# A Flamingo-style block in one kernel: PSUM banks taken in turn, bf16 pairs in the second attention's output products, and another order of the first key and query chunks

## The chip, the cores and the metric

The kernel runs on one core of one Trainium2 chip, as a single launch. The metric is the device time of that core in microseconds, as the median of several runs. A core has five engines with an instruction queue each: TensorE (PE in the profile, PEld for its weight loads), VectorE (DVE), ScalarE (ACT), GpSimd (POOL) and SyncE (SP), which starts the DMAs. They meet through semaphores only. TensorE writes to PSUM, eight banks of 128 x 512 fp32 values, called BK0 to BK7 here.

## What is computed

Four batches of 256 tokens with 256 features pass through two layers; the context has 1601 vectors of 128 features in each batch. Cut to its lines, the reference is

```
x = x + tanh(g_xattn[0]) * L0_xattn(layernorm(x), ctx)        # 16 heads of 16, normed q and k
x = x + tanh(g_ffn[0])   * L0_ffn(layernorm(x))               # 16 experts, top 8, squared relu
x = x + tanh(g_xattn[1]) * L1_xattn(layernorm(x), ctx, mask)  # 16 heads of 128, 8 key heads
x = x + tanh(g_ffn[1])   * L1_ffn(layernorm(x))               # ternary weights, silu(up) * gate

# L1_xattn, of which the change touches the last two steps
q, k, v = text @ Wq, vision @ Wk, vision @ Wv                 # k and v shared by two heads
p   = exp(q . k / sqrt(128) - max)                            # over 1601 keys
out = (p @ v) / p.sum()
return out.reshape(B, 256, 2048) @ Wo
```

## The kernel before

A planner (class `Plan`) writes one list of pieces, such as `("sc", s)` or `("o1p", g, j)`. Each engine then goes through this list and issues its own share of each piece, so that the list sets the order on every engine. `fill(bank, piece)` gives a piece a PSUM bank, and the piece waits until the last user of that bank has been read. The waits are semaphores: `filled` (TensorE has written) and `emptied` (the reader is done).

- **Start (`first_batch`)**: keys and queries of batch 0 are projected into 16 tiles, which go on in five chunks: three of four key tiles (numbers 0, 1, 2 of the code), one of two key tiles (3, the tail), and one of the two query tiles (4). Each chunk is squared on ScalarE (`sq`), summed on VectorE (`ss`), square-rooted on ScalarE (`sqrt`), scaled on VectorE (`scale`), turned by TensorE (`kt`, for queries `qt`), copied twice by ScalarE (once as bf16) and split into a bf16 pair (`ksplit`, `qsplit`, L1528 on VectorE or L2069 and L2085 on GpSimd). Then rearranging matmuls (`qr`, `kr`) bring queries and keys to their places. The queries go through this last.
- **First attention (75 to about 515 us)**: tiles of scores (`sc`), exponentials on ScalarE (L1879), products with the values, and row maxima (`mx`, L1533 on VectorE). The banks 4, 0, 5, 1, 3, 2, 7 are taken in turn by `mbank`; bank 6 accumulates. When a group of heads ends, `finish` uses bank 7 outside this turn: `oB` (four transposes; VectorE reads them in L1561), `oC`, `oD` (VectorE in L1582) and the next norm's transposes `ln`. The router and the shared expert (`routed`) use bank 3 for the first half of the tokens.
- **Experts (about 515 to 620)**: 32 steps. `up` fills banks 0 to 2 and 3 to 5 in alternation; ScalarE (L1933, L1935) and VectorE (L1660, L1664) work on them; `dn` accumulates in bank 6. Everything else goes through bank 7: `routed` of the second half, 16 times `fold` (the second attention's weights multiplied together; ScalarE reads them in L1919 and L1920, and GpSimd splits the query side M1 into a bf16 pair in L2102 and L2104), four `tl` of the first half (VectorE in L1670), and norms. The maxima of the first two query groups of the second attention follow, with `md` always in bank 4 (read in L1993) and `mb` always in bank 5 (read in L1696).
- **Second attention (about 640 to 1436)**: 32 groups g of 13 steps, one for each 128 keys (`kt` is the step in the group). A step has three or four 128x512 bf16 matmuls of scores (`s1`), exp on ScalarE (L1981), a split on GpSimd (L2141), a running sum of the exponentials on VectorE in bank 6 (L1718 and L1721), and three matmuls with the context (`v1`) into bank 2 or 3. Maxima of later groups lie between. When a group ends, ScalarE copies the products (`o1v`, L2000) and the sums (`o1s`, L2006) out as fp32; `o1a` sums over partitions with four fp32 matmuls of one column; `o1p`, twice in a group, multiplies with the folded output weights N1 in two fp32 matmuls of 256 columns each, and VectorE adds the result to x (L1735).
- **Last feed-forward (to the end)**: not touched but for what runs ahead of it.

An fp32 matmul stands in the trace as two records. TensorE's instructions carry line L732, that of the helper `mm`.

## Time and profile before

| | |
|---|---|
| Median of 3 runs | 1485.71 us (1482.29 to 1487.23) |
| Profiled execution, its time | 1487.37 us |
| Its span in the profile | 1486.1 us |
| Busy: PE, DVE, ACT, POOL | 1356.2, 1025.3, 894.9, 680.9 us |
| Mean granted TensorE clock | 0.962 |

The span begins with the first instruction and ends with the last one; 1.3 us lie around it. Times of day below are microseconds from its start. Matmuls are pipelined, so the mean time of one is longer than the distance from one to the next; the busy time of a group is that of its union. A granted clock of 1.00 is 2.4 GHz, and 0.5 would be 1.2 GHz.

### The profile page before, as it was taken

To read this page: it belongs to the slowest core of one execution; us is meant where nothing else is said; L and a number is where in the kernel's file an instruction comes from. 1 tells how busy PE (TensorE), PEld (TensorE's weight loads), DVE (VectorE), ACT (ScalarE), POOL (GpSimd) and SP (SyncE) were. 2 spreads that over 40 slices of the span, in tenths; PEclk is the share of its full clock that TensorE was granted. 3 is DMA by queue.
4 is the path that set the end of the run, shared out by engine and by line. 5 is a ranking of instruction groups with operands and counts; after the bars stand their busy time and mean duration, and the time that the engine had idled before them with its cause. 6 is when DMAs were issued, how large, how long until landed. Compare 5 with 4: busy or idle time off the path is not lost.

```text
span 1486.1 us, 24911 instructions
## 1 busy us (share of the span) xinstructions
PE 1356.2 (91%) x8524; PEld 675.7 (45%) x8524; DVE 1025.3 (69%) x2259; ACT 894.9 (60%) x1575; POOL 680.9 (46%) x753
## 2 busy tenths in 40 slices
PE   5688979889878988789999999999999999999998
PEld 4243434334333344335455545545454555454555
DVE  5677787687787256756766666756667776767656
ACT  4656657557655756366665666555665555656554
POOL 4035343243040023157655547565576565555553
PEclk8799989999989999889999999999999999999999
DMA  4000301201250100001000000000010000000000
GB/s 174 1 1 15 77 2 24 46 1 28 42 199 1 58 0 6 23 23 29 1 1 1 23 1 24 6 1 23 1 29 29 1 30 1 30 1 1 1 2 29
DMA packets 20484, 36.66 MB, mean 25 GB/s; under 512 B 4898, under 2 KB 15238, under 8 KB 19334
## 3 DMA queue, kind: packets, MB, share of 16 engines
q1 hardware_dynamic: 20358, 35.07, 8.1%
q8 instruction: 68, 1.11, 0.3%
q14 instruction: 58, 0.48, 0.1%
HBM read 26.53 MB, written 1.15 MB: 19 GB/s over the span
## 4 chain that ended last, share of the span: by engine, by line
PE 50%; issue 3%; DVE 2%; ACT 2%; POOL 2%; DVEq 0%; POOLq 0%; ACTq 0%
PE BK L732 50%; POOL arena L2141 1%; DVE arena L1696 1%; DVE arena L2330 0%; ACT arena L1981 0%; ACT arena L1993 0%; DVE arena L2336 0%; POOL arena L1104 0%; PE BK L1377 0%; ACT L1024 0%; PE BK L1051 0%; ACT arena L2362 0%; ACT arena L2366 0%; POOL arena L2132 0%; POOL arena L1102 0%
## 5 line engine op out<-in xcount | busy, mean ns | idle before, releaser
L732 PE MATMUL BK<-arena 128*128 128x512 bf16 (+13 forms) x8194 | 1314.9, 365 | 94.5 <-DVE arena L1533 17.2
L732 PEld LDWEIGHTS BK<-arena 128*128 128x128 bf16 (+7 forms) x8194 | 639.9, 110 | 737.8 <-issue 193.2
L2141 POOL TENSOR_TENSOR arena<-arena 128x512 bf16<-128x512 f32 (+1 forms) x416 | 440.0, 1062 | 244.5 <-ACT arena L1981 187.0
L1981 ACT ACTIVATE arena<-BK,arena 128x512 f32<-128x512 f32 (+1 forms) x416 | 285.7, 687 | 199.0 <-PE BK L732 193.8
L1879 ACT ACTIVATE arena<-BK 128x512 f32<-128x512 f32 (+1 forms) x416 | 222.8, 601 | 116.7 <-PE BK L732 114.4
L1533 DVE TENSOR_REDUCE arena<-BK 128x1 f32<-128x512 f32 x384 | 241.3, 683 | 59.0 <-PE BK L732 58.4
L1721 DVE TENSOR_TENSOR BK<-BK,arena 128x512 f32<-128x512 f32 (+1 forms) x352 | 244.3, 694 | 44.8 <-ACT arena L1981 41.0
L1696 DVE CUSTOM_DVE_ANT_0 arena<-BK,arena 128x512 bf16<-128x512 f32 (+1 forms) x256 | 147.2, 575 | 109.7 <-PE BK L732 106.8
L1993 ACT ACTIVATE arena<-BK 128x512 bf16<-128x512 f32 (+1 forms) x256 | 129.9, 507 | 104.6 <-PE BK L732 104.6
L1735 DVE SCALAR_TENSOR_TENSOR arena<-BK,arena 128x256 f32<-128x256 f32 x128 | 56.1, 480 | 34.8 <-PE BK L732 34.7
L2044 POOL TENSOR_TENSOR arena<-arena 128x1024 f32<-128x1024 f32 (+2 forms) x15 | 23.3, 1550 | 86.4 <-DVE arena L1475 86.4
L1660 DVE TENSOR_TENSOR arena<-BK,arena 128x512 f32<-128x512 f32 x32 | 22.0, 689 | 43.3 <-ACT arena L1935 43.2
L1724 DVE TENSOR_SCALAR arena<-BK 128x4 f32<-128x4 f32 x32 | 5.2, 163 | 62.0 <-PE BK L732 62.0
L2102 POOL CAST arena<-arena 128x256 bf16<-128x256 f32 x16 | 6.4, 397 | 79.3 <-ACT arena L1919 79.3
L2085 POOL TENSOR_TENSOR arena<-arena 128x512 bf16<-128x512 f32 (+2 forms) x32 | 26.5, 829 | 31.8 <-ACT arena L1845 29.4
L2059 POOL TENSOR_TENSOR arena<-arena 128x1024 f32<-128x1024 f32 (+2 forms) x15 | 23.2, 1580 | 37.4 <-DVE arena L982 37.4
L2147 POOL TENSOR_TENSOR arena<-arena 128x4 f32<-128x4 f32 x32 | 6.4, 199 | 57.5 <-DVE arena L1726 57.5
L2048 POOL TENSOR_TENSOR arena<-arena 128x256 f32<-128x256 f32 (+6 forms) x45 | 30.2, 671 | 3.5
L1966 ACT CAST arena<-BK 128x512 bf16<-128x512 f32 x32 | 18.8, 586 | 21.4 <-PE BK L732 21.4
L2132 POOL TENSOR_TENSOR arena<-arena 128x384 bf16<-128x384 f32 (+1 forms) x20 | 16.3, 839 | 30.5 <-ACT arena L1959 30.5
L2083 POOL CAST arena<-arena 128x512 bf16<-128x512 f32 (+2 forms) x30 | 13.5, 451 | 34.8 <-ACT arena L1835 34.3
L1718 DVE TENSOR_TENSOR BK<-arena 128x512 f32<-128x512 f32 x32 | 27.1, 848 | 2.9 <-ACT arena L2006 2.9
(184 smaller groups left out, 841.8 us busy)
## 6 DMA issues: line engine op xcount, KB each, us to landing
arena<-arena SPq DMA_DIRECT2D x144, 50.0 KB, 2.2
arena<-in_ctxT SPq DMA_DIRECT2D x8, 800.5 KB, 4.4
arena<-in_ctxk SPq DMA_DIRECT2D x4, 768.0 KB
arena<-in_wo SPq DMA_DIRECT2D x1, 2048.0 KB, 7.9
arena<-in_wqT SPq DMA_DIRECT2D x1, 2048.0 KB, 8.9
arena<-in_x SPq DMA_DIRECT2D x4, 256.0 KB, 9.7
arena<-in_rsel SPq DMA_DIRECT2D x1, 1024.0 KB, 9.4
arena<-in_rw1T SPq DMA_DIRECT2D x1, 1024.0 KB, 5.3
```

The source lines that it names most:

```text
L732: return T.matmul(out_, lhsT, rhs, start=start, stop=stop, skip_group_check=True)
L1533: V.tensor_reduce(mxp[:, g % 2, u, c:c + 1], BK[i][:, :], AX.X, ALU.max).then_inc(free[i], 1)
L1696: V.tensor_tensor_reduce(out=junk[:, 0:w], in0=BK[i][:, 0:w], in1=rl[:, k % 3, 0:w], scale=1.0, scalar=-3e38, op0=ALU.add, op1=ALU.max, ac ...
L1718: V.tensor_tensor(BK[6][:, :], P1[(s - 1) % NR][:, :], P1[k][:, :], ALU.add).then_inc(summed1, 1)
L1721: V.tensor_tensor(BK[6][0:m, :], BK[6][0:m, :], P1[k][0:m, :], ALU.add).then_inc(summed1, 1)
L1735: t = V.scalar_tensor_tensor(out=x_sb[:, k, :], in0=BK[i][:, 256 * t2:256 * t2 + 256], scalar=dn[:, 8 + u:9 + u], in1=x_sb[:, k, :], op0=A ...
L1879: A.activation(P0[(2 * s + r) % NP][0:m, :], BK[i][0:m, :], ACT.Exp, scale=0.25).then_inc(free[i], 1)
L1981: A.activation(P1[k][0:m, :], BK[i][0:m, :], ACT.Exp, scale=SCALE1, bias=mcb[0:m, b, kt:kt + 1]).then_inc(free[i], 1)
L1993: A.activation(rl[:, k % 3, 0:w], BK[i][:, 0:w], ACT.Relu).then_inc(free[i], 1)
L2048: G.tensor_tensor(sv[:, :, 0:w], sv[:, :, 0:w], sv[:, :, w:2 * w], ALU.add).then_inc(pool_chain.sem, pool_chain.up())
L2085: G.tensor_tensor(ktl[hf_][:, w_], x, kth[hf_][:, w_], ALU.subtract).then_inc(lo_pool, 1)
L2141: G.tensor_tensor(Pl[k][0:m, :], P1[k][0:m, :], Ph[k][0:m, :], ALU.subtract).then_inc(p_low, 1)
```

## The change

It has four parts.

1. **Banks.** In the first attention, `oB`, `oC`, `oD`, the norms and the first `routed` take the next bank of the running turn instead of bank 7 or 3. In the experts all pieces (`up`, `fold`, `routed`, `tl`, norms, and the maxima of query groups 0 and 1) take banks 0, 1, 2, 3, 4, 5, 7 in turn. The second attention goes on as before, but for what is left of group 1, which alternates between banks 4 and 5.
2. **Output products.** N1 is kept as a bf16 pair (N1h, N1l), which GpSimd makes after each `fold` from a staging tile; ScalarE waits for it before it stages the next. The products of a group are kept as a pair as well: ScalarE copies the high part as bf16 (`o1v`), and VectorE subtracts to get the low part in a new piece `o1w`. `o1p` is then three bf16 matmuls where one fp32 matmul stood: 6 instead of 2 of 256 columns.
3. **Sums.** The same for the sum of exponentials: ScalarE copies the high part, VectorE makes the low part in a new piece `o1t`, and `o1a` is 8 bf16 matmuls of one column instead of 4 in fp32.
4. **Start.** The queries of batch 0 are the third of the five chunks, not the last. The places of squares and sums (`TURN0`, `QTURN0`) follow.

```diff
@@ -32,6 +32,7 @@
+TURN0, QTURN0 = (0, 1, 3, 4, 2), 2
@@ -79,7 +80,7 @@
-        self.fill(7, "ln", turn, b)
+        self.fill(next(self.turn) if 0 < 4 * turn + b < 10 else 7, "ln", turn, b)
@@ -140,49 +141,49 @@
...
+            piece("scale", 0, 0)
             piece("ss", 0, 2)
             piece("sq", 0, 3)
-            yield
-            piece("ksplit", 0, 0, 0)
+            piece("ksplit", 0, 0, 1)
+            yield
+            piece("qt", 0, bank=bank())
             piece("sqrt", 0, 2)
...
@@ -302,15 +303,16 @@
-            piece("oB", g, bank=7)
+            piece("oB", g, bank=next(self.turn))
             yield
             if g % 4 == 3:
-                piece("oC", g // 4, bank=7)
-                yield
-                piece("oD", g // 4, bank=7)
+                piece("oC", g // 4, bank=next(self.turn))
+                yield
+                piece("oD", g // 4, bank=next(self.turn))
...
+        self.turn = mbank
@@ -324,15 +326,15 @@
-            yield from routed(to, 0, 3)
+            yield from routed(to, 0, mbank)
@@ -408,7 +410,7 @@
-                piece("fold", h, bank=7)
+                piece("fold", h, bank=next(self.turn))
@@ -435,12 +437,13 @@
-        ends = chain(self.last, self.routed(to, 1, 7))
+        self.turn = itertools.cycle((0, 1, 2, 3, 4, 5, 7))
+        ends = chain(self.last, self.routed(to, 1, self.turn))
@@ -452,7 +455,7 @@
-                    self.fill(3 * (s % 2) + k, "up", s, k)
+                    self.fill(next(self.turn), "up", s, k)
@@ -492,11 +496,11 @@
-                self.fill(4, "md", g, k // 2, k % 2)
+                self.fill(next(self.turn) if g < 2 else 4, "md", g, k // 2, k % 2)
...
-                self.fill(5, "mb", g, (k - 1) // 2, (k - 1) % 2)
+                self.fill(next(self.turn) if g < 2 else 5, "mb", g, (k - 1) // 2, (k - 1) % 2)
@@ -566,6 +571,7 @@
             piece("o1v", g)
             piece("o1a", g, bank=7)
             yield
+            piece("o1w", g)
             yield
@@ -617,6 +623,8 @@
             pace(2)
+            if kt == 1 and s > NKT:
+                piece("o1t", g - 1)
@@ -1408,14 +1423,19 @@
                     for u in range(4):
-                        t = mm(BK[7][:, u:u + 1], acc[:, g % 2, 128 * u:128 * u + 128], ones[:, 0:1])
+                        mm(BK[7][:, u:u + 1], acch[:, g % 2, 128 * u:128 * u + 128], onb[:, 0:1], stop=False)
+                        t = mm(BK[7][:, u:u + 1], accl[:, g % 2, 128 * u:128 * u + 128], onb[:, 0:1], start=False)
...
                     pe.wait_ge(pv_taken, g + 1)
+                    pe.wait_ge(n1_split, H)
                     for t2 in range(2):
-                        t = mm(BK[i][:, 256 * t2:256 * t2 + 256], oN[:, h, 128 * t2:128 * t2 + 128], N1[:, h, :])
+                        o, tok = BK[i][:, 256 * t2:256 * t2 + 256], slice(128 * t2, 128 * t2 + 128)
+                        mm(o, oNh[:, h, tok], N1h[:, h, :], stop=False)
+                        mm(o, oNh[:, h, tok], N1l[:, h, :], start=False, stop=False)
+                        t = mm(o, oNl[:, h, tok], N1h[:, h, :], start=False)
@@ -1719,6 +1738,18 @@
+                elif kind == "o1w":
+                    g, = arg
+                    h, j = 2 * (g % 8), 2 + g % 2
+                    dve.wait_ge(pv_high, g + 1)
+                    V.tensor_tensor(oNl[:, h:h + 2, :].rearrange("p h n -> p (h n)"), BK[j][:, :],
+                                    oNh[:, h:h + 2, :].rearrange("p h n -> p (h n)"), ALU.subtract).then_inc(pv_taken, 1)
+                elif kind == "o1t":
+                    g, = arg
+                    dve.wait_ge(acc_high, g + 1)
...
+                    V.tensor_tensor(accl[:, g % 2, :], BK[6][:, :], acch[:, g % 2, :], ALU.subtract).then_inc(acc_out, 1)
@@ -1911,13 +1942,15 @@
-                    A.copy(N1[:, h, :], BK[7][:, 256:512]).then_inc(free[7], 1)
+                    if h:
+                        act.wait_ge(n1_split, h)
+                    A.copy(n1s[:, :], BK[i][:, 256:512]).then_inc(free[i], 1)
@@ -1997,13 +2030,13 @@
-                    A.copy(oN[:, h:h + 2, :].rearrange("p h n -> p (h n)"), BK[j][:, :]).then_inc(pv_taken, 1)
+                    A.copy(oNh[:, h:h + 2, :].rearrange("p h n -> p (h n)"), BK[j][:, :]).then_inc(pv_high, 1)
...
-                    A.copy(acc[:, g % 2, :], BK[6][:, :]).then_inc(acc_out, 1)
+                    A.copy(acch[:, g % 2, :], BK[6][:, :]).then_inc(acc_high, 1)
@@ -2102,6 +2135,10 @@
+                    pool.wait_ge(*emptied("fold", h))
+                    G.tensor_copy(N1h[:, h, :], n1s[:, :]).then_inc(pool_chain.sem, pool_chain.up())
+                    pool.wait_ge(pool_chain.sem, pool_chain.n)
+                    G.tensor_tensor(N1l[:, h, :], n1s[:, :], N1h[:, h, :], ALU.subtract).then_inc(n1_split, 1)
```

The first place is VectorE in the middle of a group of the second attention, before and after. L1721 (L1740 in the change) is the running sum, L1724 (L1755) reads the sums of `o1a`, L1686 (L1705) is the low part of the next queries, and L1735 (L1766) reads `o1p`.

```order
L1721 TENSOR_TENSOR BK6<-BK6,arena 128x512 x2
L1707 TENSOR_SCALAR arena<-BK7 4x128
L1721 TENSOR_TENSOR BK6<-BK6,arena 128x512
L1724 TENSOR_SCALAR arena<-BK7 128x4
L1726 RECIPROCAL arena<-arena 128x4
L1721 TENSOR_TENSOR BK6<-BK6,arena 128x512
L1686 TENSOR_TENSOR arena<-BK4,arena 128x512
L1721 TENSOR_TENSOR BK6<-BK6,arena 128x512
L1735 SCALAR_TENSOR_TENSOR arena<-BK7,arena 128x256 x2
```

```order
L1740 TENSOR_TENSOR BK6<-BK6,arena 128x512 x2
L1726 TENSOR_SCALAR arena<-BK7 4x128
L1740 TENSOR_TENSOR BK6<-BK6,arena 128x512
L1755 TENSOR_SCALAR arena<-BK7 128x4
L1757 RECIPROCAL arena<-arena 128x4
L1740 TENSOR_TENSOR BK6<-BK6,arena 128x512
L1705 TENSOR_TENSOR arena<-BK4,arena 128x512
L1745 TENSOR_TENSOR arena<-BK2,arena 128x512
L1740 TENSOR_TENSOR BK6<-BK6,arena 128x512
L1766 SCALAR_TENSOR_TENSOR arena<-BK7,arena 128x256 x2
```

In the change L1745, which is `o1w`, stands between the low part of the queries and the next running sum, ahead of the first L1766. `o1t` (L1752) is one more such instruction, ahead of the first running sum of the group.

The second place is TensorE in the experts, with bank numbers. Three rows of 512 columns are one `up`, 128x128 x2 with 128x256 is one `fold`, 64x512 is `dn` and the last row is a norm's transposes.

```order
L732 MATMUL BK5<-arena 128x512
L732 MATMUL BK6<-arena 64x512 x2
L732 MATMUL BK7<-arena 128x128 x2
L732 MATMUL BK7<-arena 128x256
L732 MATMUL BK1<-arena 128x512 x2
L732 MATMUL BK0<-arena 128x512 x2
L732 MATMUL BK2<-arena 128x512
L732 MATMUL BK7<-arena 128x128 x2
L732 MATMUL BK7<-arena 128x256
L732 MATMUL BK4<-arena 128x512 x2
L732 MATMUL BK3<-arena 128x512 x2
L732 MATMUL BK5<-arena 128x512
L1051 MATMUL BK7<-arena 128x128 x4
```

```order
L740 MATMUL BK0<-arena 128x512
L740 MATMUL BK6<-arena 64x512 x2
L740 MATMUL BK1<-arena 128x128 x2
L740 MATMUL BK1<-arena 128x256
L740 MATMUL BK2<-arena 128x512 x2
L740 MATMUL BK3<-arena 128x512 x2
L740 MATMUL BK4<-arena 128x512
L740 MATMUL BK5<-arena 128x128 x2
L740 MATMUL BK5<-arena 128x256
L740 MATMUL BK7<-arena 128x512 x2
L740 MATMUL BK0<-arena 128x512 x2
L740 MATMUL BK1<-arena 128x512
L1064 MATMUL BK2<-arena 128x128 x4
```

The order of the work is the same. Before, both folds and the norm use bank 7, and `up` alternates between two sets of three; in the change a bank comes back after seven fills, whoever uses it.

The third place is ScalarE near the end of the start, in the first batch: L1808 is a square, L1814 a square root, L1844 and L1845 the two copies of a key chunk, L1848 to L1855 those of the tail, and L1823 and L1826 those of the queries (in the change L1839, L1845, L1875 and L1876, L1879 to L1886, L1854 and L1857).

```order
L1844 ACTIVATE arena<-BK2,arena 128x512
L1845 ACTIVATE arena<-BK2,arena 128x512
L1814 ACTIVATE arena<-arena 128x32
L1848 ACTIVATE arena<-BK7,arena 128x49
L1850 ACTIVATE arena<-BK7,arena 128x49
L1853 ACTIVATE arena<-BK7,arena 128x16
L1855 ACTIVATE arena<-BK7,arena 128x16
L1823 ACTIVATE arena<-BK0,arena 128x512
L1826 ACTIVATE arena<-BK0,arena 128x512
```

```order
L1839 ACTIVATE arena<-arena 65x512
L1854 ACTIVATE arena<-BK2,arena 128x512
L1857 ACTIVATE arena<-BK2,arena 128x512
L1845 ACTIVATE arena<-arena 128x64
L1845 ACTIVATE arena<-arena 65x32
L1875 ACTIVATE arena<-BK7,arena 128x512
L1876 ACTIVATE arena<-BK7,arena 128x512
```

Before, the two copies of the queries come last; in the change they stand ahead of the third and the fourth key chunk.

## Rows read from the trace of the kernel before

**Rows 1.** The page, parts 1 and 2: busy time, and granted clock in 40 slices.

```profile
PE 1356.2 (91%) x8524; PEld 675.7 (45%) x8524; DVE 1025.3 (69%) x2259; ACT 894.9 (60%) x1575; POOL 680.9 (46%) x753
...
PEclk8799989999989999889999999999999999999999
```

**Rows 2.** Windows by stage: span; busy us (instructions) by engine; clock, DMA.

```profile
0.00:75.00 75.00, 46.96 (x204) 27.16 (x205) 47.33 (x87) 42.81 (x81) 18.99 (x27) 0.82 0.23 87
75.00:500.00 425.00, 367.19 (x3481) 160.15 (x3479) 320.38 (x658) 269.43 (x509) 138.86 (x173) 0.93 0.15 38
500.00:620.00 120.00, 101.73 (x556) 46.75 (x552) 70.56 (x145) 69.92 (x136) 27.06 (x46) 0.96 0.07 24
620.00:648.00 28.00, 21.44 (x77) 8.91 (x76) 13.30 (x41) 13.95 (x25) 6.04 (x8) 0.76 0.15 45
648.00:1400.00 752.00, 737.64 (x3770) 387.06 (x3769) 519.22 (x1238) 456.93 (x762) 452.26 (x463) 1.00 0.04 12
```

**Rows 3.** Groups by form, second attention (648 to 1400): PE matmuls.

```profile
L732 PE MATMUL BK<-arena 128*128 128x256 f32 x232 | 59.5, 379 | 0.0
L732 PE MATMUL BK<-arena 128*128 128x256 bf16 x360 | 44.2, 273 | 0.0
L732 PE MATMUL BK<-arena 128*128 128x1 f32 x238 | 28.4, 239 | 0.0
```

**Rows 4.** The same view and stretch: PE weight loads.

```profile
L732 PEld LDWEIGHTS BK<-arena 128*128 128x128 bf16 x3068 | 297.3, 98 | 333.7 <-DVE arena L1696 20.7 <-POOL arena L2141 6.0 <-ACT arena L1993 4.7
...
L732 PEld LDWEIGHTS BK<-arena 128*128 128x128 f32 x470 | 73.4, 191 | 12.1
```

**Rows 5.** The same view, 0 to 500: the shortest bf16 matmuls from 128 rows.

```profile
L732 PE MATMUL BK<-arena 128*128 128x65 bf16 x16 | 1.9, 205 | 0.0
```

**Rows 6.** The same view, 648 to 1400: VectorE, a subtraction from PSUM.

```profile
L1686 DVE TENSOR_TENSOR arena<-BK,arena 128x512 bf16<-128x512 f32 x30 | 20.4, 681 | 0.6 <-ACT arena L1966 0.6
```

**Rows 7.** Timeline around the end of one group of the second attention.

```profile
818.28 0.74 DVE L1718 TENSOR_TENSOR BK<-arena 128x512 f32<-128x512 f32 x1
...
824.61 0.59 ACT L2000 COPY arena<-BK 128x512 f32<-128x512 f32 x1
...
825.80 0.68 DVE L1686 TENSOR_TENSOR arena<-BK,arena 128x512 bf16<-128x512 f32 x1
...
826.97 0.70 DVE L1721 TENSOR_TENSOR BK<-BK,arena 128x512 f32<-128x512 f32 x1 [0.49 <-ACT arena L1981]
...
828.64 0.48 DVE L1735 SCALAR_TENSOR_TENSOR arena<-BK,arena 128x256 f32<-128x256 f32 x1 [0.97 <-PE BK L732]
```

**Rows 8.** TensorE's waits, first attention (75 to 500): total, times, longest.

```profile
PE BK L732 <- DVE arena L1561: 7.9, 4, 3.6
...
PE BK L732 <- DVE arena L1582: 3.8, 2, 2.3
```

**Rows 9.** TensorE's waits, experts (500 to 620).

```profile
PE BK L732 <- DVE arena L1670: 2.5, 2, 1.9
...
PE BK L732 <- ACT arena L1920: 1.5, 1, 1.5
```

**Rows 10.** TensorE's waits, 620 to 648: first query groups' maxima.

```profile
PE BK L732 <- DVE arena L1696: 3.2, 4, 1.6
PE BK L732 <- ACT arena L1993: 1.9, 5, 0.7
```

**Rows 11.** Timeline of the start (43 to 50): last chunks prepared.

```profile
43.69 0.18 DVE L1528 TENSOR_TENSOR arena<-arena 128x16 bf16<-128x16 f32 x1 [0.30 <-ACT arena L1855]
...
44.16 0.69 DVE L1506 TENSOR_TENSOR arena<-arena 128x512 f32<-128x512 f32 x1
...
48.90 1.44 PE L732 MATMUL BK<-arena 128*128 128x256 bf16 x5 [2.81 <-issue]
```

**Rows 12.** Groups by form, experts (500 to 620): GpSimd splitting folded weights.

```profile
L2104 POOL TENSOR_TENSOR arena<-arena 128x256 bf16<-128x256 f32 x16 | 10.7, 671 | 1.3
...
L2102 POOL CAST arena<-arena 128x256 bf16<-128x256 f32 x16 | 6.4, 397 | 79.3 <-ACT arena L1919 79.3
```

More of the change, by code:

```diff
@@ L334, in routed @@
                 if k == 2:
-                    self.fill(bank, "rt", ch)
+                    self.fill(next(bank), "rt", ch)
                     to.append(("rt", ch))
@@ L344, in routed @@
             yield
-            self.fill(bank, "wt", ch)
+            self.fill(next(bank), "wt", ch)
             to.append(("wt", ch))
@@ L462, in stage1 @@
                         pass
-                    ends = chain(tail(0, [7] * 4), self.norm(to, 2, 0), self.norm(to, 2, 1))
+                    ends = chain(tail(0), self.norm(to, 2, 0), self.norm(to, 2, 1))
                 if p % 2:
@@ L482, in stage1 @@
         piece("mcb")
+        self.ended = self.fills[:]
     def qproj(self, g, bank=4):
```

144 lines of the change are left out of this document (76 added, 68 removed).

## The prediction

> **What bounds the kernel now.** I read the page first. TensorE is busy for 91% of the span, VectorE for 69%, and the row of granted clocks has only 9s in its second half [rows 1]. The windows by stage show where TensorE really sets the time [rows 2]. In the second attention, 752 us, TensorE is busy for 737.64 us at a granted clock of 1.00 (2.4 GHz), while VectorE works 519.22 us, ScalarE 456.93 and GpSimd 452.26. So there TensorE's own work is the time, and what is taken from its stream comes off the span, if nobody else is made late. The other stages are different. In the first attention TensorE is busy for 367.19 of 425 us at 0.93; in the experts for 101.73 of 120; while the first query groups' maxima are taken (620 to 648) for 21.44 of 28 at a clock of 0.76; and at the start for 46.96 of 75. Those stages are made of chains between engines and of waits for a bank, so I read there who TensorE waits for.
>
> **The output products (o1p), second attention.** A record's mean duration includes the way through the array, so I take distances from the unions of the groups. The fp32 matmuls of 256 columns stand in groups of four records: 232 records are 58 groups, 59.5 us are 1.026 us for each, and without the last one's own 0.379 us three distances are left, 0.216 us each [rows 3]. The bf16 ones of the same width stand in groups of twelve (the query projections): 30 groups, 1.473 us each, less 0.273 us, are eleven distances of 0.109 us. Those load weights of 128x128 before each matmul too, so the load is hidden at that rate, as it will be here. One `o1p` is now 4 records of 0.216 us, 0.86 us, and becomes 6 of 0.109 us, 0.65 us: 0.21 us less. With 2 in each of 32 groups that is **13.4 us**.
>
> **The sums (o1a).** Four fp32 matmuls of one column are eight records; 238 records, some 30 groups, take 28.4 us, 0.947 us for each, less 0.239 us: seven distances of 0.101 us [rows 3]. One column is no work, so the distance is that of the weight load. In the change there are eight bf16 matmuls of one column, and the trace has none. From above, their distance is at most the same 0.101 us, and nothing is saved. From below there are the bf16 matmuls of 65 columns, 8 pairs in 1.9 us: 0.238 us for a pair, less 0.205 us, 0.03 us from one to the next [rows 5]. Between the ends I go by the loads: 98 ns for bf16 against 191 ns for fp32 [rows 4], so half of 0.101 us, 0.05 us. One `o1a` falls from 0.81 to 0.41 us, and 32 of them give **12.6 us** (0 to 18).
>
> The Trainium skill (TensorE: Matmul & The Clock Gate, "LDWEIGHTS") puts a load at its columns divided by 1.2 GHz, 107 ns, and halves this where a bf16 weight fills 128 columns ("Weight-path perf modes"). By the first figure alone `o1a` would save nothing; by both the load is 53 ns, and the sum stays where it is. No row here decides between them for one column.
>
> **What VectorE gets for it.** `o1w` and `o1t` are 64 subtractions of 128x512 from PSUM; the same form takes 681 ns in L1686 [rows 6], together 43.6 us. With 519.22 + 43.6 = 563 us in some 726 us VectorE is busy for 78% and still not the bound, so the question is only whether somebody waits at the two places. `o1w` stands behind L1686, which ends at 826.48, and ScalarE's copy L2000 is done at 825.20; the next running sum starts at 826.97 because its exp is late by 0.49 us, and the first product that VectorE reads comes at 828.64 [rows 7]. `o1w` would end near 827.2, and `o1p` starts on TensorE some 1.0 us before VectorE reads it (its 0.86 us and the signal), near 827.6: a margin of 0.4 us. If that cover were gone, TensorE would stand still in front of `o1p`, with the next step's `s1` behind it, and so ScalarE's exp and everything after. `o1t` pushes L1718 (818.28) and the last maximum back by 0.68 us; the running sum has the idle time up to 828.64 to catch up. I charge both with nothing in the middle of the stage. In the last group no maxima of a next one give cover, and the chain from the last `v1` to the norm gets one or both subtractions, at most 1.4 us: I take **+1 us**.
>
> **The banks.** In the first attention TensorE waits 7.9 us for VectorE's L1561 and 3.8 us for L1582 [rows 8]. Both free bank 7 after `oB` and `oD`, and those who wait are score tiles whose turn happens to come to bank 7. In the change they get the bank that was used longest ago. But VectorE came late to L1561 because it was behind with maxima, and the tiles behind them need it too, so I count a third: **-4 us** (0 to -12). In the experts a `fold` waits for bank 7 behind a `tl` (L1670, 2.5 us) or behind the last `fold` (L1920, 1.5 us) [rows 9]: **-4 us** (0 to -8, if still other users of that bank gain). The reuse of `up`'s banks gets closer, from two steps to seven fills, some one and a half steps with a `fold` and a piece of `routed` between; 32 steps share 101.73 us of TensorE's work [rows 2], 3.2 us each, and relu, square and the two VectorE products of 0.7 us each fit into it. In the maxima of groups 0 and 1, each `md` has waited for ScalarE to empty bank 4 and each `mb` for VectorE to empty bank 5, 1.9 and 3.2 us [rows 10]. With seven banks TensorE runs ahead and VectorE sets the pace: I take **-3 us** of the 5.1 (0 to -8, with the half clock of that stretch).
>
> **The split of N1.** GpSimd does a cast of 397 ns and a subtraction of 671 ns for each `fold` [rows 12], and now twice of both, 2.1 us. In the 120 us of the experts it was busy for 27.06 us [rows 2], and 16 x 1.07 = 17 us are added. ScalarE waits for the last N1 split before it stages the next; 16 folds spread over 16 steps of over 3 us, so this costs nothing on the mean. Where two come closer together than 2.1 us, ScalarE stands for some tenths; I leave that in the range.
>
> **The start.** Before, behind the last key split (43.69 + 0.18 us) came the queries' scaling (44.16), their transposes, two copies, a split on GpSimd, and only at 48.90 the first rearranging matmul: 5.0 us [rows 11]. In the change this runs in the middle, where VectorE and ScalarE have gaps, but its VectorE work and the waits for the queries' copies push the last key chunk back. I count half: **-2.5 us** (0 to -5).
>
> **The sum.** -13.4 - 12.6 + 1 - 4 - 4 - 3 - 2.5 = -38.5 us. From the profiled execution's time of 1487.4 us that is 1448.9; the median of the runs shown is 1.7 us below that execution, so I predict **1447 us**.
>
> **The rivals.**
>
> *The banks are not what holds TensorE* (chance 0.15). Each wait for a bank moves to the next dependency, VectorE's backlog, since VectorE works as much as before. Then only the second attention and the start pay: -26 + 1 - 2.5, 1458 us. For it: VectorE is busy for 320.38 of 425 us in the first attention [rows 2]. Against it: folds and `tl` depend on nothing but the bank.
>
> *VectorE's new work stalls TensorE in every group* (0.10). If `o1w` comes 0.4 us after TensorE has reached `o1p`, 0.8 us later than I read it, 32 groups give 13 us back: 1460 us. The margin of 0.4 us is from one group, and batch norms make some groups worse.
>
> *The banks give more* (0.12). All of the 11.7 us in the first attention, 8 us each in the two stages after it, partly as less time at half clock: another 17 us or so, 1430 us. For it: clocks of 0.93 and 0.76 [rows 2].
>
> *Turning through the banks costs the clock* (0.03), the other side. If TensorE stops briefly and often at each bank's turn, the clock in the experts falls. At 0.5 instead of 0.96 the 101.73 us of work take 195 us, 75 more than the whole stage's 120: 1447 + 75 = 1522 us, slower than before. It decides once that stage's clock falls below 0.62, where 101.73 x 0.96 / 0.62 = 158 us eat up the 38.5 us. Against it: the first attention already takes seven banks in turn and has 0.93, the experts without it 0.96.
>
> The Trainium skill describes this (TensorE: Matmul & The Clock Gate, "A second HAM failure mode: psum-queue depth-cycling"): cycling through PSUM banks in each iteration made TensorE idle briefly between groups so often that the clock went up and down. By that rule the kernel would come out near 1522 us; the trace's 0.93 speaks against the full effect.
>
> **How the numbers follow.** The forecast gets 0.60, with a range of its own of 1438 to 1456. From its bounds alone, `o1a` without any gain gives 1460 us and all gains at their upper ends some 1421 us. The range of **1432 to 1463 us** takes in the first two rivals, and leaves out most of the third and the fourth. Under 0.3%, 4.5 us, this kernel can't be told from an unchanged one. Only the fourth rival is slower (0.03); no change (0.02) would need the second rival's stalls three times as long; the rest is faster (0.95).
>
> **What would show it.** In the profile after: in the second attention two L1718 (one in each group) 0.8 us nearer to each other than before; TensorE still busy for 98% there; 8 one-column records in about 0.6 us of union; no wait of TensorE for `o1w`; no waits for `oB`'s and `oD`'s readers of over 1 us in front of score tiles; the first rearranging matmul near 46.4 us. Wrong would be: TensorE waiting for the new subtractions in most groups, a one-column distance that stays at 0.10 us, or a clock below 0.9 in the experts.

## The result, and the profile after

The changed kernel takes 1442.03 us (median of 4 runs, 1438.38 to 1445.58), beside 1484.14 us for the kernel before on the same chip: a ratio of 0.9714, with an interval of [0.9678, 0.975]. In a second set of five rounds it was 0.9694 [0.9674, 0.9714]. The forecast was 1447 us, its range 1432 to 1463. The profiled execution shown below took 1445.6 us, its span is 1444.2 us.

The page after, parts 1 and 2, beside [rows 1]:

```profile
PE 1328.7 (92%) x8652; PEld 646.2 (45%) x8652; DVE 1083.1 (75%) x2323; ACT 894.2 (62%) x1575; POOL 700.1 (48%) x785
...
PEclk9788998999989999899999999999999999999999
```

TensorE has 27.5 us less to do, VectorE 57.8 us more. The windows by stage, beside [rows 2]:

```profile
0.00:75.00 75.00, 49.89 (x223) 27.83 (x223) 51.39 (x95) 47.45 (x92) 18.64 (x27) 0.86 0.23 87
75.00:500.00 425.00, 378.12 (x3615) 165.17 (x3616) 315.90 (x655) 275.28 (x520) 139.15 (x173) 0.92 0.16 42
500.00:620.00 120.00, 101.57 (x449) 50.78 (x448) 79.66 (x167) 67.07 (x130) 46.88 (x82) 0.90 0.04 14
620.00:648.00 28.00, 26.55 (x126) 12.26 (x125) 18.79 (x46) 19.57 (x34) 16.41 (x18) 0.94 0.09 31
648.00:1400.00 752.00, 731.94 (x3995) 366.20 (x3994) 586.00 (x1317) 462.99 (x770) 464.99 (x475) 1.00 0.04 12
```

The windows are cut at the same times, and the work has moved ahead: 620 to 648 us already holds second-attention work. So I compare by landmarks, the starts of the same instruction in both traces. "First oA" and "last oA" are the first and last of ScalarE's sixteen L1885 (after: L1916), at the end of a group of heads; E1 and E31 are the first exponential (L1981, L2014) of query groups 1 and 31 of the second attention, so that thirty groups lie between them.

| us | first oA | last oA | E1 | E31 | span | E1 to E31 |
|---|---|---|---|---|---|---|
| before | 116.58 | 511.23 | 665.73 | 1414.41 | 1486.1 | 748.69 |
| after | 116.44 | 497.96 | 645.25 | 1372.90 | 1444.2 | 727.65 |
| after, second set | 112.42 | 495.72 | 641.10 | 1368.74 | 1439.4 | 727.64 |

Half of the gain, 20.5 us, is there before group 1; 21.0 us come in the thirty groups. The last column is a sharp measure: in two executions of the changed kernel it is equal within 0.01 us, while E1 differs by 4 us. I use it below.

One thing has to be allowed for. In eight of the fourteen executions traced here, these three among them, TensorE's clock falls to half (a granted clock of 0.5, 1.2 GHz) for 3.4 us between the first exponentials of groups 8 and 9. In the other six it doesn't (s_prod, a_late, a_one, a_nolow, b_exp and a_two_late, all below). The window from group 8 to group 9 in s_banks and in b_exp, which run the same work there:

```profile
817.21:848.39 31.18, 27.62 (x134) 14.06 (x133) 20.73 (x52) 20.67 (x33) 13.66 (x14) 0.95 0.08 27
```

```profile
828.48:857.99 29.51, 25.95 (x134) 13.55 (x133) 20.73 (x52) 20.67 (x32) 13.66 (x14) 1.00 0.09 29
```

The stretch costs 1.67 us, and it is the whole difference between the last columns of the two, 748.76 and 747.10 us. So the kernel before, without it, takes 747.10 us. For the changed kernel I estimate 726.2: its group 8 takes 30.15 us, a_late's 28.50, of which the gap found below explains 0.19, and 1.46 are left. Where one kernel of a pair has the stretch and the other not, I give both differences.

**First attention and experts.** TensorE's waits, 75 to 500 us, beside [rows 8]:

```profile
PE BK L740 <- DVE arena L1553: 20.5, 23, 4.3
PE BK L1239 <- DVE arena L1566: 8.9, 5, 2.6
```

The waits for the readers of `oB` (L1561, 7.9 us) and `oD` (L1582, 3.8 us) are gone. The waits for the maxima (L1553, before L1533) and for their reduction (L1566, before L1546) grew at the same time, from 16.3 and 3.3 us to 20.5 and 8.9; what is left as a gain is seen in the landmarks, 13 us by the last oA. In the experts, beside [rows 9], neither `tl` (now L1689) nor a `fold` is waited for. The first ones are now a norm, 6.8 us where it was 3.2, and an `up`, as before:

```profile
PE BK L1064 <- DVE arena L1027: 6.8, 3, 3.3
PE BK L740 <- ACT arena L1966: 3.1, 2, 1.8
```

**Second attention.** Groups by form, 648 to 1400 us, beside [rows 3]: matmuls, the load for `m1n`, and VectorE's first running sum (L1737, before L1718).

```profile
L740 PE MATMUL BK<-arena 128*128 128x1 bf16 x256 | 10.9, 164 | 0.2 <-DVE arena L1752 0.2
...
L1391 PEld LDWEIGHTS BK<-arena 128*4 128x4 f32 x30 | 2.5, 82 | 15.7 <-issue 12.5 <-DVE arena L1781 2.9
...
L1737 DVE TENSOR_TENSOR BK<-arena 128x512 f32<-128x512 f32 x31 | 46.5, 1499 | 4.1
```

256 records are the 32 `o1a`, 0.341 us each; less the 0.164 us of the last one, seven distances of **0.025 us**. The prediction had 0.05. Eight of them are 0.20 us where 0.81 us stood, 0.61 us less in a group. In the kernel before, the same two other groups were:

```profile
L1377 PEld LDWEIGHTS BK<-arena 128*4 128x4 f32 x31 | 2.6, 85 | 4.4 <-issue 0.9
...
L1718 DVE TENSOR_TENSOR BK<-arena 128x512 f32<-128x512 f32 x31 | 26.1, 841 | 0.0
```

So the weight load of `m1n` (the transpose of a group's maxima, L1377 or L1391) comes after 15.7 us of idle time of its queue instead of 4.4, of which the matmuls feel a part, and the same sum of two tiles takes 1.50 instead of 0.84 us. The timeline of the changed kernel at the end of a group shows both:

```profile
792.89 0.69 DVE L1752 TENSOR_TENSOR arena<-BK,arena 128x512 bf16<-128x512 f32 x1
...
793.69 1.04 POOL L2178 TENSOR_TENSOR arena<-arena 128x512 bf16<-128x512 f32 x1 [0.61 <-ACT arena L2014]
793.71 1.57 DVE L1737 TENSOR_TENSOR BK<-arena 128x512 f32<-128x512 f32 x1
...
795.20 0.45 DVE L1715 CUSTOM_DVE_ANT_0 arena<-BK,arena 128x289 bf16<-128x289 f32 x1
...
795.69 0.16 DVE L1721 TENSOR_REDUCE arena<-arena 128x4 f32<-128x8 f32 x1
...
795.96 0.08 PEld L1391 LDWEIGHTS BK<-arena 128*4 128x4 f32 x1 [0.50 <-issue]
```

`o1t` (L1752) puts the running sum behind the start of GpSimd's split (L2178), by 0.02 us. It then takes 1.57 us, the last maximum (L1715) and its reduction (L1721) come late, and TensorE, which turns just that result in `m1n`, starts it 0.413 us behind its last matmul of 512 columns, where the others follow in 0.215: 0.20 us lost. Before, the sum began at 818.28 [rows 7], when the split of that step had 0.18 us left, and took 0.74 us:

```profile
817.42 1.04 POOL L2141 TENSOR_TENSOR arena<-arena 128x512 bf16<-128x512 f32 x1 [0.61 <-ACT arena L1981]
```

### The profile page after: what moved, and what is told of

Its sections match the earlier page's. It is cut to its first block, busy times and chain, and to the rows that moved or that the text cites. A ratio compares the mean times of both kernels' runs of the same rounds, so it can differ in the third digit from the quotient of the medians.

```text
span 1444.2 us, 25271 instructions
## 1 busy us (share of the span) xinstructions
PE 1328.7 (92%) x8652; PEld 646.2 (45%) x8652; DVE 1083.1 (75%) x2323; ACT 894.2 (62%) x1575; POOL 700.1 (48%) x785
## 4 chain that ended last, share of the span: by engine, by line
PE 48%; DVE 4%; issue 3%; ACT 2%; POOL 2%; DVEq 0%; POOLq 0%; ACTq 0%
PE BK L740 47%; DVE arena L1715 2%; POOL arena L2178 1%; ACT arena L2014 1%; PE BK L1391 1%; DVE arena L2367 0%; DVE arena L2373 0%; DVE BK L1740 0%; ACT arena L2026 0%; ACT L1034 0%; POOL arena L1117 0%; POOL arena L2169 0%; PE BK L1064 0%; ACT arena L2399 0%; POOL arena L1115 0%
## 5 line engine op out<-in xcount | busy, mean ns | idle before, releaser
L740 PE MATMUL BK<-arena 128*128 128x512 bf16 (+11 forms) x8322 | 1286.2, 359 | 72.4 <-DVE arena L1553 21.1
L740 PEld LDWEIGHTS BK<-arena 128*128 128x128 bf16 (+7 forms) x8322 | 612.1, 104 | 709.4 <-issue 206.8
L2178 POOL TENSOR_TENSOR arena<-arena 128x512 bf16<-128x512 f32 (+1 forms) x416 | 441.9, 1067 | 226.9 <-ACT arena L2014 175.3
L2014 ACT ACTIVATE arena<-BK,arena 128x512 f32<-128x512 f32 (+1 forms) x416 | 285.7, 687 | 186.8 <-PE BK L740 183.0
L1553 DVE TENSOR_REDUCE arena<-BK 128x1 f32<-128x512 f32 x384 | 240.7, 681 | 51.2 <-PE BK L740 50.6
L1740 DVE TENSOR_TENSOR BK<-BK,arena 128x512 f32<-128x512 f32 (+1 forms) x352 | 243.7, 692 | 16.1 <-ACT arena L2014 10.4
L1715 DVE CUSTOM_DVE_ANT_0 arena<-BK,arena 128x512 bf16<-128x512 f32 (+1 forms) x256 | 147.0, 574 | 102.4 <-PE BK L740 99.2
L1766 DVE SCALAR_TENSOR_TENSOR arena<-BK,arena 128x256 f32<-128x256 f32 x128 | 55.8, 476 | 15.0 <-PE BK L740 15.0
L1680 DVE TENSOR_TENSOR arena<-BK,arena 128x512 f32<-128x512 f32 x32 | 22.0, 687 | 38.9 <-ACT arena L1968 38.8
L1737 DVE TENSOR_TENSOR BK<-arena 128x512 f32<-128x512 f32 x32 | 47.5, 1484 | 4.1
L2081 POOL TENSOR_TENSOR arena<-arena 128x256 f32<-128x256 f32 (+6 forms) x45 | 30.3, 672 | 3.5
L1821 ACT COPY arena<-BK 128x512 f32<-128x512 f32 x24 | 14.1, 586 | 26.5 <-PE BK L740 26.3
L1495 DVE TENSOR_TENSOR arena<-BK,arena 128x512 f32<-128x512 f32 (+1 forms) x28 | 19.2, 687 | 13.7 <-PE BK L740 13.4
```

The costliest lines, as they stand in the source:

```text
L740: return T.matmul(out_, lhsT, rhs, start=start, stop=stop, skip_group_check=True)
L1553: V.tensor_reduce(mxp[:, g % 2, u, c:c + 1], BK[i][:, :], AX.X, ALU.max).then_inc(free[i], 1)
L1715: V.tensor_tensor_reduce(out=junk[:, 0:w], in0=BK[i][:, 0:w], in1=rl[:, k % 3, 0:w], scale=1.0, scalar=-3e38, op0=ALU.add, op1=ALU.max, ac ...
L1737: V.tensor_tensor(BK[6][:, :], P1[(s - 1) % NR][:, :], P1[k][:, :], ALU.add).then_inc(summed1, 1)
L1740: V.tensor_tensor(BK[6][0:m, :], BK[6][0:m, :], P1[k][0:m, :], ALU.add).then_inc(summed1, 1)
L1766: t = V.scalar_tensor_tensor(out=x_sb[:, k, :], in0=BK[i][:, 256 * t2:256 * t2 + 256], scalar=dn[:, 8 + u:9 + u], in1=x_sb[:, k, :], op0=A ...
```

## The experiments

Ratios are to the kernel before, measured beside each, with 95% intervals. The four parts come first, each made alone in the kernel before (1488.09 us beside them).

**s_start**, part 4 alone:

```diff
+TURN0, QTURN0 = (0, 1, 3, 4, 2), 2
...
+            piece("scale", 0, 0)
+            piece("ksplit", 0, 0, 1)
+            piece("qt", 0, bank=bank())
```

> The kernel before with part 4 of the change alone (queries of batch 0 third of five chunks). Theory A, the gain of the start is real but doesn't reach the end: in the changed kernel the first rearranged queries came 5.7 us earlier and keys 4.4 us earlier, but at 95 us nothing of it was left, in a stretch at half clock (80.7 to 94.3 us) that the kernel before doesn't have there. If the half clock comes from the start's own order of work, this kernel has it too, is 4 to 5 us ahead at 75 us and 0 to 1 us at the first group of heads' end, and its total lies within 1.5 us of before. Theory B, as predicted (the start passes its gain on): 2 to 5 us faster in the total, because the half clock near 81 us has to do with the banks and is not in this kernel.

Measured: 1486.05 us, 0.9997 [0.9977, 1.0018]. The first rearranged queries came 5.5 us earlier, the first oA 0.6 us later; the traced execution has a half clock from 80.9 us for 13.7 us. That agrees with A in the total, though the interval (3.4 us less to 2.7 more) also takes in the lower part of B. But the cause that A names, the new order of the start, is wrong, as the later kernels show: the changed kernel, its second trace and the five variants of it below run the same instructions up to 600 us. Windows of 75 to 100 us of the kernel before, the changed kernel, and a_two (below):

```profile
75.00:100.00 25.00, 20.30 (x146) 9.35 (x145) 21.08 (x41) 15.11 (x31) 6.63 (x7) 1.00 0.01 2
```

```profile
75.00:100.00 25.00, 21.87 (x126) 10.00 (x127) 16.36 (x34) 10.58 (x20) 6.32 (x6) 0.73 0.00 1
```

```profile
75.00:100.00 25.00, 21.06 (x159) 10.89 (x159) 19.68 (x39) 12.46 (x23) 9.14 (x10) 1.00 0.00 1
```

The granted clock is 0.73 in one and 1.00 in the other, for the same program. And b_att (below), with the old order of the start, has a half clock from 84.2 us. In the five executions of the seven without the half clock there the first oA stands at 111.7 to 112.9 us, 4 us ahead of before; in the two with it at 116.3 and 116.4. With the old order it stands at 116.0 to 116.7, and with b_att's half clock at 118.6. So the start's gain is there at the first oA where no half clock falls behind it, and is gone where one does. How much of it comes through to the end, the totals don't show; of the ten executions of s_start one has a trace.

**s_banks**, part 1 alone:

```diff
-            piece("oB", g, bank=7)
+            piece("oB", g, bank=next(self.turn))
...
-                    self.fill(3 * (s % 2) + k, "up", s, k)
+                    self.fill(next(self.turn), "up", s, k)
```

> The kernel before with part 1 alone (banks). Theory A, the banks are what held TensorE outside the second attention: from the changed kernel's landmarks (13 us gained in the first attention, 3 in the experts, 4 in the maxima of groups 0 and 1) the total is 17 to 21 us shorter, some 1465 us, and the waits for the readers of oB and oD are gone. Theory B (the prediction's sum): 11 us shorter, some 1474 us, the rest of the gain in the first attention coming from the start's new order. Theory C (the prediction's first rival): less than 3 us, the waits go over to the maxima.

Measured: 1468.82 us, 0.9877 [0.9853, 0.9901], 18.3 us less (14.7 to 21.9). A holds, B and C fall. From first to last oA it takes 381.3 us (before 394.7), from there to E1 145.8 (154.5), from E1 to E31 748.8, as before.

**s_prod**, part 2 alone:

```diff
-                        t = mm(BK[i][:, 256 * t2:256 * t2 + 256], oN[:, h, 128 * t2:128 * t2 + 128], N1[:, h, :])
+                        mm(o, oNh[:, h, tok], N1h[:, h, :], stop=False)
+                        mm(o, oNh[:, h, tok], N1l[:, h, :], start=False, stop=False)
+                        t = mm(o, oNl[:, h, tok], N1h[:, h, :], start=False)
```

> The kernel before with part 2 alone (output products in bf16 pairs, o1w, split of N1 on GpSimd). Theory A (the prediction's term stands): 64 x 0.21 = 13.4 us less in the second attention, total 1471 us, o1w hidden in all groups. Theory B (part of it goes into waits): as read from the changed kernel, up to 12 us of the two parts' gains in the second attention are given back; if o1w had a share in that, this kernel gains 8 us or less, 1476 us.

Measured: 1476.9 us, 0.9934 [0.9918, 0.9951], 9.8 us less (7.3 to 12.2). E1 to E31 takes 735.05 us, without the half-clock stretch: 13.64 less than before, 12.05 less than 747.10. That is 0.40 us for each group where 0.42 was forecast; in a group without anything special, 24.52 us became 24.11. So A holds in the stage itself, with next to nothing given back to `o1w`. The total by itself would be B's 1476 us. The trace doesn't show where the rest went: it is that of the fastest of the four executions (1472.97 us), and its E1 is 0.8 us ahead of before. I can't name it.

**s_sums**, part 3 alone:

```diff
-                        t = mm(BK[7][:, u:u + 1], acc[:, g % 2, 128 * u:128 * u + 128], ones[:, 0:1])
+                        mm(BK[7][:, u:u + 1], acch[:, g % 2, 128 * u:128 * u + 128], onb[:, 0:1], stop=False)
+                        t = mm(BK[7][:, u:u + 1], accl[:, g % 2, 128 * u:128 * u + 128], onb[:, 0:1], start=False)
```

> The kernel before with part 3 alone (sum of exponentials in bf16 pairs, o1t). The stream of TensorE loses 32 x 0.61 = 19.5 us by the distance of 0.025 us that the changed kernel shows for one column. Theory A (o1t delays the next running sum into GpSimd's split, so that it takes 1.57 instead of 0.74 us and VectorE comes late to m1n): 32 x 0.2 = 6.4 us and some more are given back, 11 to 13 us are left, 1472 us, and L1718's running sum of step 1 takes about 1.5 us. Theory B (the waits come from both subtractions together): the running sum keeps 0.85 us or is stretched but nobody waits, and the full 19 us come, 1465 us.

Measured: 1477.45 us, 0.9931 [0.9912, 0.995], 10.3 us less. E1 to E31 takes 739.11 us, 9.6 less (both with the half-clock stretch), while the stream alone would give 30 x 0.61 = 18.3; 8.7 us are given back. The view of one line (shortest, median, longest of 32, ns; first and last start) for the running sum:

```profile
L1722 DVE TENSOR_TENSOR BK<-arena x32: 700/1571/2272, 649.4 to 1410.7; 128x512 f32<-128x512 f32 x32
```

A holds: `o1t` alone makes it 1.57 us (before: median 0.736). The four parts by themselves add up to 38.8 us, the whole change gave 42 to 46.

The next three change one thing in the changed kernel; before took 1487.84 us beside them.

**a_late**, `m1n` half a step later:

```diff
         self.main.append(("mf", g))
         yield
         yield
         yield
+        yield
         self.fill(7, "m1n", g)
         self.main.append(("m1n", g))
-        yield
         self.rowed.add(g)
```

> The changed kernel with m1n, the transpose of a query group's maxima, one of the half steps later (L1391 on TensorE behind one more piece of its work). Theory A (TensorE's recurring gap of 0.20 us in front of m1n is lost time): the gap goes, and 30 x 0.2 = 6 us come off, some 1436 us against the changed kernel's 1442; ratio to before 0.968. Theory B (another queue is the bound in that place, so the wait moves on to the next instruction that needs VectorE or GpSimd): the same 1442 us within 1.5.

Measured: 1438.35 us, 0.9668 [0.9637, 0.9698]. E1 to E31 takes 720.93 us, 6.7 less than in the changed kernel, 5.3 less without its half-clock stretch (A: 6), and the load of `m1n` is no longer late:

```profile
L1391 PEld LDWEIGHTS BK<-arena 128*4 128x4 f32 x30 | 2.5, 83 | 5.0 <-DVE arena L1781 0.9 <-issue 0.8
```

A holds in the stage; in the total the interval touches that of the changed kernel.

**a_one**, first running sum from one SBUF tile; the other tile, 128 of the keys, is left out of the sum:

```diff
-                        V.tensor_tensor(BK[6][:, :], P1[(s - 1) % NR][:, :], P1[k][:, :], ALU.add).then_inc(summed1, 1)
+                        V.tensor_copy(BK[6][:, :], P1[k][:, :]).then_inc(summed1, 1)
```

> The changed kernel, with the first running sum of each group reading one SBUF tile instead of two (a copy into the bank; the first 128 keys are left out of the sum of exponentials). Theory A (VectorE's instruction with two SBUF inputs is held while GpSimd's split works on SBUF): the instruction falls from 1.48 us in the mean to 0.75 or less though it starts at the same place in GpSimd's work, the wait in front of m1n shrinks from 0.20 us to nothing, and the total falls by 4 to 6 us to some 1437 us. Theory B (it is held by something else, such as PSUM bank 6 that ScalarE or VectorE has just read): it still takes over 1.2 us, and the total stays at 1442 us.

Measured: 1434.59 us, 0.9642 [0.961, 0.9673]; E1 to E31 717.44 us, 10.2 less than in the changed kernel, 8.7 without its half-clock stretch. The timeline:

```profile
788.89 1.04 POOL L2178 TENSOR_TENSOR arena<-arena 128x512 bf16<-128x512 f32 x1 [0.61 <-ACT arena L2014]
```

```profile
788.09 0.69 DVE L1752 TENSOR_TENSOR arena<-BK,arena 128x512 bf16<-128x512 f32 x1
788.91 0.69 DVE L1737 COPY BK<-arena 128x512 f32<-128x512 f32 x1
```

It begins 0.02 us behind the start of GpSimd's split, exactly as the sum does in the changed kernel, writes the same bank, and takes 0.69 us. So it is neither the bank nor the subtraction just before it. Nor is it that a copy stands where an addition stood. The changed kernel's other running sums add the bank and one SBUF tile; 52 of them begin with over 0.9 us of a split ahead, and none takes over 0.70 us:

```profile
L1740 DVE TENSOR_TENSOR BK<-BK,arena x352: 678/691/700, 628.8 to 1391.1; 128x512 f32<-128x512 f32 x160, 65x512 f32<-65x512 f32 x16
```

It is the instruction with two SBUF inputs that is held. The Trainium skill (SBUF — State Buffer, "SBUF: two separate sides") states this: VectorE with two SBUF inputs and a GpSimd instruction that reads SBUF take a shared pair of ports as an exclusive lock, and the later one waits. By that rule the sum would begin at the split's end, 793.69 + 1.04 = 794.73, and with its own 0.70 us (its shortest in the row of s_sums) end at 795.43; the trace has 795.28. It agrees but for 0.15 us. In the kernel before, the sum at 818.28 would by the same rule end at 818.46 + 0.70 = 819.16, and ends at 819.02, 0.14 us sooner: so there it was held too, by 0.04 us.

**a_nolow**, without `o1t`; the low part is left out, and TensorE multiplies the high part twice, so that its work stays the same:

```diff
-            if kt == 1 and s > NKT:
-                piece("o1t", g - 1)
...
-                        t = mm(BK[7][:, u:u + 1], accl[:, g % 2, 128 * u:128 * u + 128], onb[:, 0:1], start=False)
+                        t = mm(BK[7][:, u:u + 1], acch[:, g % 2, 128 * u:128 * u + 128], onb[:, 0:1], start=False)
```

> The changed kernel without o1t (the low part of the sum of exponentials is left out; TensorE multiplies the high part twice, so its work is the same). Theory A: the first running sum is back at some 0.73 us, the wait in front of m1n is gone, and 6 us or somewhat more come off, 1435 us; that is the full price of o1t, which the prediction had at nothing. Theory B (o1t has nothing to do with the waits): 1442 us, the waits in front of m1n stay.

Measured: 1435.47 us, 0.9645 [0.9614, 0.9675]; E1 to E31 716.80 us. A holds, the price is larger: 10.85 us in thirty groups, 9.4 without the changed kernel's half-clock stretch. From 747.10 us it is 30.3, and 12.05 + 18.3 is 30.35: without `o1t` the whole gain of TensorE's stream comes through. And all but 0.64 us of this price also goes with a_one (717.44 against 716.80, both without the stretch), which keeps `o1t`'s 0.69 us of VectorE: the subtraction itself costs next to nothing, the place into which it pushes the sum costs nearly everything.

Of the next four, two split the banks and two mend the sum; before took 1488.86 us beside them.

**b_att** and **b_exp**, the turning banks in the first attention alone, and in the experts and first maxima alone. Against s_banks:

```diff
-        self.turn = itertools.cycle((0, 1, 2, 3, 4, 5, 7))
+        self.turn = itertools.repeat(7)
...
-                    self.fill(next(self.turn), "up", s, k)
+                    self.fill(3 * (s % 2) + k, "up", s, k)
```

```diff
-        self.turn = mbank
+        self.turn = itertools.repeat(7)
...
-            yield from routed(to, 0, mbank)
+            yield from routed(to, 0, itertools.repeat(3))
```

> The kernel before with the turning banks in the first attention alone (oB, oC, oD, its norms and the first routed); experts and maxima of groups 0 and 1 use their fixed banks. In the kernel with all of part 1 the last normalised group's sum (L1885's last place) came 13.6 us earlier than before. Theory A (this gain is the banks' there, and it is all handed through): 13 us less in the total, 1475 us where before has 1488. Theory B (most of it is eaten later, since the stage after it starts at another point of VectorE's and the clock's work): 8 us less or fewer. Theory C (the prediction): 4 us less, 1484 us.

> The kernel before with the turning banks in the experts and in the maxima of groups 0 and 1 alone; the first attention uses bank 7 and bank 3 as before. With all of part 1 the time between the end of the first attention and the first exponentials of the second attention fell by another 8 us. Theory A (the gain of the two places adds up): 5 to 8 us less in the total, 1481 us where before has 1488, close to the prediction's 4 + 3. Theory B (the experts had no gain of their own from banks, only the first attention's gain came on): less than 3 us.

Measured: b_att 1479.0 us, 0.9936 [0.9912, 0.9959], 9.5 us less (6.1 to 13.1); b_exp 1479.45 us, 0.9932 [0.9909, 0.9955], 10.1 us less (6.7 to 13.5). Together 19.6 us, both at once 18.3: they add up, and b_exp's theory B falls. For b_att the interval reaches A's 13 and B's 8 and leaves out the forecast's 4. Its waits for 75 to 500 us:

```profile
PE BK L736 <- DVE arena L1540: 23.7, 23, 4.7
...
PE BK L1231 <- DVE arena L1553: 7.7, 5, 2.6
```

The 11.7 us of waits for `oB`'s and `oD`'s readers [rows 8] are gone, and the waits for maxima and their reduction grew from 16.3 and 3.3 us to these 23.7 and 7.7: sums of waits don't tell the gain, the landmark (394.7 to 384.9 us from first to last oA) does. For b_exp, from last oA to E1 the 154.5 us became 145.2; its trace also lacks the half-clock stretch, 1.6 us from E1 to E31 that are not the banks'.

**a_two**, first running sum in two instructions of one SBUF input each, and **a_two_late**, the same with a_late's edit:

```diff
-                        V.tensor_tensor(BK[6][:, :], P1[(s - 1) % NR][:, :], P1[k][:, :], ALU.add).then_inc(summed1, 1)
+                        V.tensor_copy(BK[6][:, :], P1[(s - 1) % NR][:, :]).then_inc(dve_chain.sem, dve_chain.up())
+                        dve.wait_ge(dve_chain.sem, dve_chain.n)
...
+                        V.tensor_tensor(BK[6][:, :], BK[6][:, :], P1[k][:, :], ALU.add).then_inc(summed1, 1)
```

> The changed kernel with the first running sum in two instructions, each with one SBUF input: a copy of the first tile of exponentials into bank 6, then the sum with the second. Theory A (only an instruction with two SBUF inputs is held by GpSimd): each takes 0.69 us, 1.38 together where 1.50 stood, TensorE's gap in front of m1n becomes smaller by 0.1 us, and the second attention from the 14th to the 404th exponential takes 724 us (727.65 in the changed kernel, 717.44 with one instruction left out); total some 1438 us. Theory B (the length of the stretch doesn't matter, an earlier start of the copy does all or nothing): 727 us or 717 us there.

> The changed kernel with both: the first running sum in two instructions, and m1n half a step later. Theory A (what o1t costs is the time that VectorE loses in the stretch behind it): the second attention from the 14th to the 404th exponential takes 717 to 720 us (720.93 with m1n later alone), total 1434 to 1437 us, the fastest full version. Theory B (with m1n later nothing waits for the running sum any more): 721 us, the same as with m1n later alone.

In both, the copy also waits for its own tile of exponentials only, no longer for the second. That moves its start little: it comes 0.79 us behind `o1t`'s, where the sum came 0.82 behind.

Measured: a_two 1435.25 us, 0.9645 [0.9625, 0.9664]; E1 to E31 721.46 us, 6.2 less than the changed kernel (both with the half-clock stretch) where 3.6 were expected. VectorE's timeline in it:

```profile
788.65 0.69 DVE L1755 TENSOR_TENSOR arena<-BK,arena 128x512 bf16<-128x512 f32 x1
789.44 0.69 DVE L1735 COPY BK<-arena 128x512 f32<-128x512 f32 x1
790.17 0.70 DVE L1740 TENSOR_TENSOR BK<-BK,arena 128x512 f32<-128x512 f32 x1
790.77 0.45 DVE L1715 CUSTOM_DVE_ANT_0 arena<-BK,arena 128x289 bf16<-128x289 f32 x1
```

From 789.44 to the next maximum at 790.77 it is 1.33 us, in the changed kernel 795.20 - 793.71 = 1.49: two instructions are faster than one that is held. The 0.16 us cover nearly the whole gap of 0.20 us. a_two_late: 1441.56 us, 0.9673 [0.9646, 0.9701]; E1 to E31 718.62 us (without the half-clock stretch), the shortest of the full versions there, as A expected, but its total is no better. Two of its five executions took 1434.1 and 1435.3 us, three 1441.6 to 1444.0 at a mean granted clock of 0.954 or 0.955; these three have no trace, so where they lost it stays open. a_two is the fastest full version that can be told from the changed kernel.

**r_after**, the changed kernel once more:

> The changed kernel itself once more, in five rounds, as the measure for the variants of it. Theory A (the two variants with the first running sum in two instructions and with m1n later are really faster): ratio to before 0.969 to 0.972, above 0.9645 and 0.967; the second attention from the 14th to the 404th exponential takes 727.65 us again, within 0.3. Theory B (the differences between the variants are those of chips and clock phases): a ratio near 0.966. For the start: the first oA stands at 112.8 us if there is no half clock between 75 and 95 us in this execution, and at 116.4 if there is.

Measured: 1441.62 us, 0.9694 [0.9674, 0.9714], above all of a_two's interval; E1 to E31 727.64 us; no half clock between 75 and 95 us, and the first oA at 112.42. All as A said. a_late and a_two_late, though, can't be told from it by their totals.

## Why the prediction came out right, point by point

- **Output products, 13.4 us**: right. 12.05 us in thirty groups between executions at the same clock, which makes 12.9 for all 32. The margin of `o1w` held: TensorE waits for it (L1745) once, 1.1 us.
- **Sums, 12.6 us, VectorE's new work at nothing**: both wrong, and they nearly cancel. The distance was halved too little (0.025, not 0.05 us), so that the stream lost 19.5 us. But "the running sum has the idle time up to 828.64 to catch up" asked only how busy VectorE is. I moved L1718 by 0.68 us and did not look at what GpSimd does at the new time, nor at who waits for the maximum behind it. Cost: 9.4 us in thirty groups (8.7 in s_sums). Net 9.6 there.
- **First attention, 4 us**: the step that failed most. Counting "a third" for VectorE's backlog was too careful; it gave 9.5 us (6.1 to 13.1).
- **Experts and first maxima, 4 + 3 us**: 10.1 us (6.7 to 13.5), somewhat more than the sum of 7 and inside the two ranges (0 to 8 each). The split of N1 costs nothing that shows: from last oA to E1 s_prod takes 153.4 us, before 154.5.
- **Start, 2.5 us**: the chain got shorter by more (the first rearranging matmul at 42.23 us instead of 48.90, where 46.4 was forecast; the first rearranged queries are copied out at 44.29 instead of 49.95), the total by 0.4 us (3.4 less to 2.7 more). The profile after lost it again at the half clock from 81 us.
- **End, +1 us**: nothing. From the start of the last exponential of the second attention to the end of the span it is 53.1 us before, and 53.8 us in the profile after; but in the second trace of the changed kernel it is 53.1 us again, with a granted clock of 1.00 in the 8 us where the first one has 0.79. The 0.7 us are the clock's.
- **The sum**: -38.5 forecast, -41.8 between the two profiled executions. That it came so near is in part luck: by the single experiments the banks gave 18.3 us where 11 were forecast, the products 9.8 for 13.4, the sums 10.3 for 12.6 and the start 0.4 for 2.5. The errors have both signs and leave 38.8.
- **Rivals.** "Banks not the cause" fell (s_banks, both halves). "VectorE stalls TensorE in each group" was right in kind and wrong in place: not `o1w` in front of `o1p`, but `o1t` in front of `m1n`, with 0.20 us in a group, not 0.4. "The banks give more" came true by half. "Turning costs the clock": the experts' clock went from 0.96 to 0.90, 0.92 with the banks alone, far from the 0.62 at which it decides; over whole executions s_banks has 0.961 to 0.966 where the kernel before has 0.955 to 0.963. What the prediction weighed there by a rule of the Trainium skill, no run here shows at a size that costs time.

Of what would show it: the distance between two L1718 fell from 24.52 to 23.69 us; TensorE is busy for 97% there; no wait over 1 us for the readers of `oB` and `oD` is left. The eight records took 0.34, not 0.6 us.

## What to carry to other kernels

When an engine has idle time, an added instruction may still not be free: look at what starts on the other engines at the time to which it pushes its successors, above all where VectorE has two SBUF inputs and GpSimd works, and at the first one that TensorE needs. A bank that is fixed for one kind of work can cost much of the waits that stand at it; giving it to the common turn brought 18 us here without touching any work. Where half-clock stretches make a stage's time scatter, compare between landmarks inside the full-clock stage: 0.01 us between two executions here, against 4 us or more in the total. But look at the granted clock between the landmarks first: a single half-clock stretch of 3.4 us made 1.5 to 1.7 us there, as much as some of the effects that were looked for.

## What the runs showed of the hardware

- A VectorE sum with two SBUF inputs that begins 0.02 us behind a GpSimd subtraction of 1.04 us takes 1.57 us instead of 0.70; with one input, at the same distance, 0.69. Of 352 sums that read a bank and one SBUF tile none takes over 0.70 us.
- bf16 matmuls of one column with a load of 128x128 before each follow each other in 0.025 us, a quarter of fp32's 0.101 per record. The Trainium skill (TensorE: Matmul & The Clock Gate, "LDWEIGHTS" and "Weight-path perf modes") gives 53 ns for such a load, as an estimate from its two figures; a load of that length can't be what sets the distance here, and the measurement decides.
- Where the half clock falls is not fixed by the program: seven executions of the same instructions ahead of 600 us reached the last oA between 494.1 and 504.0 us. Inside the second attention, a half-clock stretch of 3.4 us lengthens the same work by 1.67 us (s_banks against b_exp).
